# Sums of exponentials in an attention over heads: two of five units on VectorE instead of TensorE

## The reference, cut to what matters

```python
def _L3_xattn_ref(Query, Key, Value, Wq, Wk, Wv, Wo):
    ...
    scores = jnp.einsum('bhqd,bhkd->bhqk', q, k) / jnp.sqrt(jnp.float32(DK))
    attn = jax.nn.softmax(scores, axis=1)
    ctx = jnp.einsum('bhqk,bhkd->bhqd', attn, v)
    ctx = ctx.transpose(0, 2, 1, 3).reshape(b, -1, H * DK)
    return ctx @ Wo.T
```

## Time and profile before

| | us |
|---|---|
| median of 3 runs | 1716.65 (1713.23 to 1717.23) |
| profiled execution, its own time | 1716.05 |
| its span in the profile | 1714.3 |
| TensorE busy | 1489.7 (87%) |
| VectorE busy | 975.5 (57%) |
| ScalarE busy | 689.8 (40%) |
| GpSimd busy | 632.9 (37%) |

### The profile page before, as it was taken

The page is one execution under the profiler, slowest core; times in us unless marked ns, Lnnn a source line. Parts: engine busy times, 40 slices in busy tenths (PEclk is TensorE's granted clock), DMA queues, the critical chain, the costliest instruction groups (busy, mean ns, idle before and its releaser), DMA issues. The chain is left out here.

```text
span 1714.3 us, 24764 instructions
## 1 busy us (share of the span) xinstructions
PE 1489.7 (87%) x9503; PEld 753.6 (44%) x9503; DVE 975.5 (57%) x1762; ACT 689.8 (40%) x1203; POOL 632.9 (37%) x646
## 2 busy tenths in 40 slices
PE   7878786898889998899878998899999879799985
PEld 4355543343334443443334535544444333355542
DVE  4798756777542212677446762454565344478845
ACT  2444322676721000477223773244434332355520
POOL 1487725543331221331103403633422213266741
PEclk8989997999989999899997998899999969989988
DMA  3000010000020000000010002000000000000000
GB/s 105 1 1 0 1 46 1 1 1 2 1 78 1 0 0 26 25 2 1 10 42 9 2 2 45 1 1 2 2 2 1 15 16 0 7 1 2 2 2 25
DMA packets 17239, 20.66 MB, mean 12 GB/s; under 512 B 7819, under 2 KB 13179, under 8 KB 16488
## 3 DMA queue, kind: packets, MB, share of 16 engines
q1 hardware_dynamic: 17128, 19.13, 3.7%
HBM read 17.94 MB, written 1.05 MB: 11 GB/s over the span
## 5 line engine op out<-in xcount | busy, mean ns | idle before, releaser
L1799 DVE CUSTOM_DVE_ANT_0 P<-P,L2f_mask 128x128 f32<-128x128 f32 (+3 forms) x256 | 118.5, 522 | 124.0 <-PE P L1702 124.0
L113 PE MATMUL P<-identb 128*128 128x512 bf16 x547 | 128.4, 391 | 3.2 <-PEq L87 3.2
L1051 DVE TENSOR_REDUCE L0f_nm<-P 128x2 f32<-128x768 f32 (+3 forms) x88 | 97.5, 1120 | 49.2 <-PE P L955 49.1
L1974 PE MATMUL P<-L0m_hm,L0m_w 128*128 128x512 f32 x256 | 111.9, 596 | 0.0
L1775 ACT ACTIVATE L2f_prob<-P 128x1024 f32<-128x1024 f32 x80 | 80.6, 1025 | 75.0 <-PE P L1714 75.0
L1007 ACT ACTIVATE L0f_prob<-P 128x512 f32<-128x512 f32 x160 | 86.9, 607 | 35.2 <-PE P L966 33.8
L1631 POOL TENSOR_SCALAR_AFFINE_SELECT L2f_prob<-L2f_prob 128x512 f32<-128x512 f32 x64 | 39.9, 638 | 162.5 <-ACT L2f_prob L1775 162.5
L1702 PE MATMUL P<-L2f_ks,L2f_qs 48*128 48x512 f32 (+3 forms) x512 | 90.8, 466 | 0.3 <-DVE L2f_nm L1799 0.3
L113 PEld LDWEIGHTS P<-identb 128*128 128x128 bf16 x547 | 54.5, 101 | 75.2 <-issue 19.6
L1714 PE MATMUL P<-L2f_qs,L2f_ks 49*128 49x256 f32 (+3 forms) x512 | 84.6, 444 | 3.1 <-DVE L2f_nm L1799 2.2
L2299 POOL TENSOR_TENSOR L3x_exm<-L3x_exm,L3x_rec 128x2048 f32<-128x2048 f32 x16 | 72.4, 4529 | 26.7 <-DVE L3x_rec L2475 26.7
(11 more groups left out here) (577 smaller groups left out, 3316.9 us busy)
## 6 DMA issues: line engine op xcount, KB each, us to landing
L0m_w<-in_L0m_w SPq DMA_DIRECT2D x1, 2048.0 KB, 7.9
L0f_va<-in_L0f_va SPq DMA_DIRECT2D x3, 512.0 KB, 4.7
in_xt<-in_x SPq DMA_DIRECT2D x1, 1024.0 KB
L0x_segi<-in_segb SPq DMA_DIRECT2D x1, 1024.0 KB, 5.2
L0m_w<-in_L0m_w SPq DMA_DIRECT2D x1, 1024.0 KB, 9.9
out<-out_o SPq DMA_DIRECT2D x4, 256.0 KB, 2.4
L1x_va<-in_va SPq DMA_DIRECT2D x3, 256.0 KB, 3.2
L1x_vr<-in_vr SPq DMA_DIRECT2D x3, 256.0 KB, 4.5
```

Of the source, the lines that this page charges most:

```text
L113: nc.tensor.matmul(G["P"][:, bank, :].rearrange("p (n c) -> p n c", n=4), G["identb"][:], G["identb"][:].unsqueeze(1).to_broadcast([128, 4 ...
L1051: nc.vector.tensor_reduce(S.nm[:, qt, first:first + 2 * many].rearrange("p (i e) -> p e i", e=2), P[:, bank:bank + 2, 0:many * width].rear ...
L1799: m = nc.vector.tensor_tensor_reduce(out=at, in0=at, in1=mask[:, T - width:T], scale=1.0, scalar=-3.0e38, op0=ALU.add, op1=ALU.max, accum_ ...
L1974: m = mm(P[:, slot(b, i) + part, :], w1[:, e, part * 512 + i * 128:part * 512 + i * 128 + 128], hm[b % 2][:, e, :], start=e == 0, stop=e = ...
```

## The change

In units 1 and 3 of each batch TensorE no longer makes the sum: T1 and T3 fall away. In their place, R1 and R3 reduce the 16 exponentials of a unit straight out of SBUF in one VectorE instruction, 2048 elements to 128, with the heads as the inner axis of reading, so that successive elements lie 128 elements apart. These reductions wait for the second half of the unit's exponentials; the others wait for TensorE's sum as before, with a count that leaves the two units out. Units 0, 2 and 4 are as before.

```diff
--- before.py
+++ after.py
@@ -2193,6 +2193,7 @@
     RING = ("q", "kv", "t1", "tk", "out")
     BY_DVE = ("out",)
     BANKS = (5, 7)
+    BY_REDUCE = (1, 3)
 
     def __init__(self, ph, G, keys, order):
         self.ph, self.G, self.nc, self.P = ph, G, ph.nc, G["P"]
@@ -2349,7 +2350,7 @@
                                 elif n == 0:
                                     m = mm(out[32 * qt:32 * qt + 32], S.ks[b % 2][rows, pair, 128:PAD], q, start=True, stop=True)
                         m.then_inc(*S.s_full.up())
-                elif kind == "sum":
+                elif kind == "sum" and n not in S.BY_REDUCE:
                     u = 5 * b + n
                     if u:
                         pe.wait_ge(S.rec_ready.sem, u)
@@ -2468,8 +2469,12 @@
                                                 ALU.subtract).then_inc(*S.sub_done.up())
                 elif kind == "rec":
                     u = 5 * b + n
-                    dve.wait_ge(S.sum_full.sem, u + 1)
-                    link(dve, nc.vector.tensor_reduce(S.tot[:], P[:, 4, :].rearrange("p (x q) -> p q x", x=4), AX.X, ALU.add), S.vstep)
+                    if n in S.BY_REDUCE:
+                        dve.wait_ge(S.exp_done.sem, 2 * u + 2)
+                        link(dve, nc.vector.tensor_reduce(S.tot[:], S.ex_of(b, n)[:].rearrange("p h q -> p q h"), AX.X, ALU.add), S.vstep)
+                    else:
+                        dve.wait_ge(S.sum_full.sem, (QT + 1 - len(S.BY_REDUCE)) * b + sum(i not in S.BY_REDUCE for i in range(n + 1)))
+                        link(dve, nc.vector.tensor_reduce(S.tot[:], P[:, 4, :].rearrange("p (x q) -> p q x", x=4), AX.X, ALU.add), S.vstep)
                     if u > 1:
                         dve.wait_ge(S.p_ready.sem, u - 1)
                     nc.vector.reciprocal(S.rec[u % 2][:], S.tot[:]).then_inc(*S.rec_ready.up())
```

## The result

The changed kernel took 1734.55 us in the median of four runs (1731.3 to 1737.86), the kernel before 1716.94 us beside it: a ratio of 1.0108, with a 95% interval of 1.0084 to 1.0131. It is slower, by 17.6 us. The forecast was 1729, with a range of 1714 to 1740.

The account below looks back on a forecast made before the run. TensorE and VectorE were taken as nearly level, with VectorE becoming the bound. Full-clock schedule +1.5, slow T2 +3.7 and slow T4 +7.9 made +13 us on 1716.05, giving 1729, range 1714 to 1740.

Parts of the forecast that it names:

- T2: TensorE's sum of unit 2: slow clock, 5.8 us long, delaying VectorE 1.35 in batches 1 and 2, about 1.0 in the last.
- T4: TensorE's sum of unit 4: slow clock, uncovered; 2.1 us into batches 1 and 2, 1.6 into batch 3, 2.1 at the end.
- The reductions: VectorE's sums of units 1 and 3: 2.29 us each, 1.6 more a unit, 3.2 a batch.
- the jumping row: Profile row of an SBUF reduction jumping from element to element: 368 ns for 192, read as nearly no jump penalty.
- The upper bound of 2.5 us: Upper price for one new reduction, from the SBUF slope of about 1.1 ns an element plus 0.13 for jumping.
- The rival of the dear reduction: Each new reduction costs 2.6 us more, held by GpSimd or slowed by reading order: 20 on top, 1749 us; chance 0.08.
- VectorE's schedule: Steps between VectorE's maxima at full clock: batch 2 sums to 36.9 us, VectorE the bound from unit 2's maximum on.
- Output projection and V1: TensorE work that, at the lower clock, could hold the next scores 2.2 us in batches 1 and 2; taken as 0.
- The new wait: The new reductions' wait for the second half of the unit's exponentials: costed at nothing.
- The signs: Expected marks: eight reductions of 2.2 to 2.5 us, TensorE's batch 2 busy time down 7, slow clock in two sums.
- The rival in which the clock holds: Unit 2's and unit 4's sums stay at 3.7 us, stage +1.5, 1717.6 us, not slower; chance 0.20.
- the sum at full clock: Stage total without clock loss: 1.75 − 2.2 − 0.8 + 2.75 = +1.5 us over the four batches.

Follow-up runs that it names:

- e1: Changed kernel with the new reductions reading 2048 elements in the order they lie (wrong elements summed): 2.28 us each, 1726.62 us, ratio 1.0054 to the kernel before.
- e2: Changed kernel with 132 elements from head to head in place of 128 (step 528 bytes): reduction 3845 ns, ratio 1.0131 to the kernel before.
- e6: Changed kernel with unread identity products in some of TensorE's pauses and reductions reading in order: stage 156.88 us, ratio 1.0027 to the kernel before.
- e9: As e6, with more unread products, most of them in the last batch: stage 157.54 us, ratio 1.0051 to the kernel before.
- e4: Changed kernel with the new reductions reading only 4 of 16 heads (512 elements): stage 161.59 us, ratio 1.0048 to the kernel before.
- e8: Kernel before with only unit 4 summed by VectorE, its buffer laid out with heads innermost: stage 158.87 us, ratio 1.0024 to the kernel before.

## Why the prediction was right, and which term was off

The direction and the mechanism held: TensorE's 29 us bought nothing, VectorE became the bound, and the clock fell at T2. That the time lies in the range is luck in part: the range had left out a dearer reduction, its upper end was made of slow sums and a held S0, and what filled it was the reduction, less an error of the other sign at T4. By its own steps, in us over what stood before:

| | predicted | measured |
|---|---|---|
| batch 0 | +1.75 | +3.87 |
| batch 1 | −2.2 + 1.35 + 2.1 = +1.25 | +5.71 |
| batch 2 | −0.8 + 1.35 + 2.1 = +2.65 | +3.74 |
| last batch | 2.75 + 1.0 + 1.6 + 2.1 = +7.45 | +7.86 |
| stage | +13.1 | +21.2 |

- **The reductions: the term that was mis-sized.** "I take 2.29 us" is what e1 measured for reading in order (2.28), and it is wrong for the order that the change uses: 3.67 us, 8 × 1.38 = 11.0 us more. The step that failed is the choice of row: the maximum "with the same order of reading, but from PSUM", and the jumping row, whose elements lie 64 bytes apart where the change's lie 512. The upper bound of 2.5 us came from that second row and was too low. (That row also has 3 elements to a total where the change has 16; which of the two differences matters no run shows. And its "25 ns over that slope" does not come out of the two rows given: 192 elements at 1.13 ns make 218 of its 368 ns, and how much of the rest is a fixed cost they do not tell.) The Trainium skill (SBUF — State Buffer, the note on cachelines) spoke against the change there, and I sided with the row. e1 and e2 agree with the page that jumps cost in SBUF, though its rule by itself does not tell the 64-byte row from the 512-byte one. The rival of the dear reduction had this mechanism as one of its two, at nearly twice the size (2.6 us each); its other, a VectorE held by GpSimd, did not occur.
- **VectorE's schedule.** In batch 2 the steps were forecast as 9.95 (M0 to M1, 7.85 and a slow T4), 6.44, 7.87, 7.55 (6.2 and a slow T2) and 8.5; they were 8.09, 6.44, 9.19, 7.90 and 9.74. The two steps with a reduction are 1.3 and 1.2 over, which is the term above; nothing else in VectorE's order was far off in this batch. In batch 1, M0 to M1 took 11.19 for 9.95: batch 0 has no addition to end it, so T4 began 0.14 us after M0 and not 0.6 before it.
- **T2.** Forecast at 5.8 us from a late start, holding R2 for 1.35, 1.35 and 1.0 us; it took 6.50, 6.13 and 5.11, and R2 waited 2.06, 1.69 and 0.66 us: 4.4 for 3.7.
- **T4.** Forecast slow each time, 7.9 us; it took 6.25 us into batch 1, 3.70 into batches 2 and 3, and 5.68 at the end: (6.25 − 3.70) + (5.68 − 3.70) = 4.5. This error has the other sign; it took back 3.4 of the 11.0 us.
- **Output projection and V1** ran slow in batches 1 and 2 as feared, yet M0 followed the addition without a wait (1623.78 above): 0 was right, and the cover was the long R3.
- **The new wait**, for the second half of the exponentials, cost nothing: 0.0 us ahead of all eight.
- **The signs.** Two of those named did not come: the reductions lay outside 2.2 to 2.5 us, and TensorE's busy time in batch 2 fell by 1.3 us (37.27 to 36.01) instead of 7. The 7 is the sums' time at full clock and leaves out what the forecast itself added for the clock.
- **The rival in which the clock holds** is out in the changed kernel. e6 and e9 come near it: in order and with fillers the stage comes to +6.4 and +7.0 (some 1.8 of the latter for the fillers themselves), where the sum at full clock said +1.5. What is left between is not settled; T2 still took 4.18 to 5.67 us in the first three batches of both.

How much each cause makes up can't be told as a sum, since they feed each other: a long reduction makes TensorE wait, a TensorE that waits can lose its clock (the last batch shows it), and slow sums make VectorE wait again. By whole times, which take in several executions, reading in order alone is worth 0.54% (1.0108 to 1.0054), fillers alone nothing that can be told (1.0091 and 1.0112), and both together 0.57 to 0.81% (e9, e6). Taken away first or second, the order of reading gave more than the fillers (6.6 against 0.2 us of the stage first, 14.6 against 8.2 second), but fillers did not give back the whole clock. So both causes are shown, the order by e1, and the clock by the slow sums of e4 and their return to full speed in e9's last batch; which of them costs more, and how much, is left open.

On the clock, the Trainium skill (TensorE: Matmul & The Clock Gate, the table of what matters for kernels) puts drops down to idle gaps. The last batch agrees with it: in the changed kernel T2 and T4 stood there behind pauses of 3.89 and 6.94 us and took 5.11 and 5.68, and once e9 had filled the pauses they took 3.70 and 3.60. The T2 of e9's batch 1, at 5.67 us behind key turns with no pause over 0.38 us in the 7 us before, and the earlier trace rows do not follow from it.

## What to carry to other kernels

Price a reduction by its step in memory as well as by its element count, and look for a row of the trace with the same memory and the same step; here a row with a shorter step was no bound from above. When two engines are nearly level, work taken from one and put on the other appears in the time nearly whole: compare what the receiving engine's idle time can lose with what its busy time gains. And before dense products are taken off TensorE, ask what stands in their place, since the products that stay may pay for it at half the clock, as the sums T2 and T4 did in e4.

## What the hardware showed that had not been expected

- VectorE's sum of 2048 fp32 elements out of SBUF takes 2.28 us in order and 3.67 with a step of 512 bytes (3.85 with 528), while its maximum out of PSUM takes 2.26 with that same step of 512, and the sum of 512 elements with that step 0.69 us out of PSUM and 1.05 out of SBUF. The price of the jump is SBUF's, some 0.68 ns an element.
- The same kind of price was met by TensorE. In e8 the values' product reads its moving operand out of SBUF with 64 bytes between elements, and 16 products (32 records) took 1.95 us against 1.08 in order, at a granted clock of 1.00 for that stretch:

```profile
1595.22:1597.09 1.87, 1.87 (x33) 1.05 (x32) 1.65 (x2) 0.24 (x1) 1.87 (x2) 1.00 0.00 0
```

- GpSimd's normalisation, on the other hand, got faster with the heads innermost, where each reciprocal repeats over 16 elements in a row: 3678 ns against 4527 in the same run.
